# Two batches of x, the gate's weights and the tables are asked for later in the start-up of a hybrid attention and expert kernel

## The reference

```
x = x + attn_a(layernorm(x))   # 16 heads; q and k of width 8 + 32 rotary-like features r, v of width 8, softmax, Wo
x = x + ffn(layernorm(x))      # gate softmax over 8 experts, top 1, silu(x W1 + b1) W2 + b2, times the gate's weight
x = x + attn_b(layernorm(x))   # 16 heads, two softmaxes of width 8 per head, rotary tables, probs = p1 - lam * p2
x = x + ffn(layernorm(x))
```

## Time and profile before

| what | value |
| --- | --- |
| median of 3 runs | 1569.77 us (1566.09 to 1571.79) |
| the profiled execution's own time | 1582.06 us |
| its span | 1580.3 us |
| mean granted TensorE clock | 0.962 |
| PE busy | 1425.1 us (90%) |
| DVE busy | 1170.7 us (74%) |
| ACT busy | 1078.4 us (68%) |
| POOL busy | 704.4 us (45%) |
| DMA | 192.78 MB, mean 122 GB/s |

### The profile page before, as it was taken

How to read it: one execution, slowest core, us unless ns; L and a number is a source line. 1 busy time by engine, 2 the same in 40 slices (tenths; PEclk the granted TensorE clock), 3 DMA queues, 4 the chain that set the end, 5 groups by cost and what they waited for, 6 DMA issues and landing times.

```text
span 1580.3 us, 27271 instructions
## 1 busy us (share of the span) xinstructions
PE 1425.1 (90%) x9388; PEld 614.0 (39%) x9388; DVE 1170.7 (74%) x2030; ACT 1078.4 (68%) x1807; POOL 704.4 (45%) x770
## 2 busy tenths in 40 slices
PE   3999999999999998999999999998898889999946
PEld 1333333335554332555443223222232225554536
DVE  4777788777777678567777888788889895677234
ACT  1576666766655776777787787687877777777712
POOL 3412533342414755675648652242521017755633
PEclk8999999999999998999999998799999998999969
DMA  6674455756734145875211210201202044523222
GB/s 190 196 208 136 138 172 163 238 170 202 222 94 103 54 154 166 259 234 171 89 36 35 87 41 21 75 28 42 61 21 80 23 157 157 167 86 126 95 102 82
DMA packets 123743, 192.78 MB, mean 122 GB/s; under 512 B 16392, under 2 KB 91938, under 8 KB 123606
## 3 DMA queue, kind: packets, MB, share of 16 engines
q1 hardware_dynamic: 114296, 176.69, 37.7%
q0 software_dynamic: 6016, 12.71, 2.3%
q10 hardware_dynamic: 3294, 1.64, 0.4%
HBM read 120.59 MB, written 71.81 MB: 122 GB/s over the span
## 4 chain that ended last, share of the span: by engine, by line
PE 67%; DVE 11%; ACT 6%; issue 5%; POOL 5%; DMA 4%; SPq 0%; ACTq 0%; POOLq 0%; DVEq 0%
PE ps L1142 19%; PE ps L1108 11%; PE ps L1129 10%; DVE Mb L1485 7%; PE ps L1239 5%; PE ps L1226 5%; ACT P L1333 5%; PE ps L1076 4%; PE ps L1150 2%; POOL ROW L1399 2%; PE ps L1223 2%; DMA xs<-ROW,slot 1%; PE ps L1237 1%; PE ps L1176 1%; POOL rs L1708 1%
## 5 line engine op out<-in xcount | busy, mean ns | idle before, releaser
L1485 DVE TENSOR_REDUCE Mb<-ps 128x2 f32<-128x1024 f32 (+1 forms) x950 | 940.6, 1015 | 254.1 <-PE ps L1108 248.8
L1333 ACT ACTIVATE P<-ps 128x512 f32<-128x512 f32 (+1 forms) x1089 | 804.7, 774 | 225.3 <-PE ps L1129 214.2
L1108 PE MATMUL ps<-STK 32*128 32x512 f16 (+1 forms) x1536 | 412.2, 391 | 44.6 <-DVE Mb L1485 16.4
L1129 PE MATMUL ps<-STK 32*128 32x512 f16 (+1 forms) x1536 | 422.8, 389 | 29.3 <-ACT P L1333 18.6
L1142 PE MATMUL ps<-P,V 128*32 128x512 f32 x3072 | 420.7, 620 | 3.5 <-ACT P L1333 3.0
L1108 PEld LDWEIGHTS ps<-STK 32*128 32x128 f16 (+1 forms) x1536 | 103.7, 94 | 295.4 <-issue 99.5
L1129 PEld LDWEIGHTS ps<-STK 32*128 32x128 f16 (+1 forms) x1536 | 108.6, 94 | 257.5 <-issue 80.3
L1753 POOL DMA_INDIRECT xs<-ROW,slot x64 | 63.3, 989 | 126.9 <-DVE slot L1575 111.0
L1760 POOL TENSOR_TENSOR TH<-TH,Z 128x512 f32<-128x512 f32 x58 | 73.6, 1269 | 88.6 <-ACT Z L1379 88.3
L1142 PEld LDWEIGHTS ps<-P,V 128*32 128x32 f32 x3072 | 61.1, 109 | 116.0 <-issue 97.5
L1226 PEld LDWEIGHTS ps<-XT,WE 128*128 128x128 f32 x696 | 93.9, 196 | 4.1
(11 more groups left out here) (169 smaller groups left out, 1433.7 us busy)
## 6 DMA issues: line engine op xcount, KB each, us to landing
WE<-in_we SPq DMA_DIRECT2D x87, 576.0 KB, 4.2
STK<-qka SPq DMA_DIRECT2D x62, 480.0 KB, 6.1
qka<-HL SPq DMA_DIRECT2D x96, 256.0 KB
STK<-qkb SPq DMA_DIRECT2D x64, 256.0 KB, 2.6
qkb<-HL SPq DMA_DIRECT2D x96, 128.0 KB
X<-xs SPq DMA_DIRECT2D x77, 129.5 KB, 3.0
xs<-pad SPq DMA_DIRECT2D x8, 1036.0 KB, 8.1
qka<-HL SPq DMA_DIRECT2D x48, 128.0 KB
```

The lines of the kernel that those rows point to most:

```text
L1108: mm = eng.matmul(ps[:, bank + i, :], l_, r_, start=True, stop=True)
L1129: mm = eng.matmul(ps[:, bank + i, :], l_, r_, start=True, stop=True)
L1333: eng.activation(P[:, st % 3, j:j + n, :], ps[:, bank:bank + n, :], ACT.Exp, scale=SCALE_A if g < 4 * B else SCALE_B).then_inc(sem("exp"), 1)
L1485: eng.tensor_reduce(Mb[:, g % 2, at:at + 4 * n - 3:4], ps[:, bank:bank + n, :], AX, ALU.max).then_inc(sem("mx"), 1)
```

## The change

In `setups()`, the job that orders the loads, setup(4), setup(5) and setup(6) wait in the plan for the end of stack(0). No instruction is added or taken away and no semaphore wait is added: only the orders that `schedule()` writes out change.

```diff
@@ -363,6 +363,8 @@
         for i, n in enumerate((1, 4, 1, 1, 1, 1, 5, 2, NS, 4, 2)):
             if i == 3:
                 yield from after(("setup", (2,)))
+            if i in (4, 5, 6):
+                yield from after(("stack", (0,)))
             if i == 8:
                 yield from after(("mput", (3,)))
             yield from do(ranks[i], "setup", i, us=0.6 * n)
```

## The result

| | kernel before | changed kernel |
| --- | --- | --- |
| median | 1570.78 us (4 runs, 1566.09 to 1581.8) | 1592.8 us (4 runs, 1589.2 to 1600.57) |
| profiled execution: own time, span, mean granted clock | 1582.06, 1580.3, 0.962 | 1593.27, 1591.5, 0.957 |
| busy PE, DVE, ACT, POOL | 1425.1, 1170.7, 1078.4, 704.4 us | 1421.4, 1169.3, 1079.3, 704.7 us |

The ratio is 1.0111, 95% interval 1.006 to 1.0161: slower, as forecast, and by more. The medians are 22 us apart (17 by the ratio) and the two profiled executions 11.2 us. Forecast were 11.7 us; 1592.8 lies above the range, which ended at 1586.

What follows compares the result with a forecast made beforehand. The start was taken as bound by DMA up to 36 us, then by DVE's rowmax. Loads 0, late x 10.75 and clock 1.0 gave +11.7 us on the 1569.77 median: 1581.5 us, range 1573 to 1586.

Steps and rivals of the forecast that it cites:

- What bounds the kernel now: Start of the kernel: DMA sets the pace up to 36 us, then DVE's ten rowmax, 11.41 us, from 37.11 to 48.5.
- What moving the loads gives: nothing.: At put(0): x loads and tables ahead held up neither its issue nor its data; 0 us, at most -1.3.
- put(4) and put(5), a gain that nobody waits for: SP's queue: these puts leave some 2 us earlier, unread by group 0; stack(0) up to 0.5 us later at no cost.
- x of batch 2 is late: DVE's rowmax wait behind ln_stats for x, landing at 47.3, and for POOL; seventh rowmax and feat(6) 10.75 us later.
- TensorE's clock: PE's stall of 8 us halves the clock for part of the feat; +1.0 us after slack at stack(4), ends 0 and +4.
- What stays hidden: Later stack(3), WG, CS and ln_apply(3) cost 0, covered by other work; uncovered, stack(3) would cost 4 us.
- The sum: Whole kernel: 0 + 10.75 + 1.0 = +11.7 us, on the median of 1569.77 giving 1581.5 us.
- x past the stacks: Rival: SP's queue order does not bind, x lands at 40.5; +3.9 us less up to 1.2, 1572.5 to 1574; chance 0.12.
- the loads were not in the way: Denies the rival that the loads held up group 0, a 1.3 us gain, alone 1568.5; chance of a gain 0.02.
- Absorbed later: Rival: slack in groups 1 to 3 shrinks the +11.7 to a few us; chance 0.07.
- Longer than forecast: Rival: clock at 0.50 for all feat and x issues held by a full queue; 3 to 5 us more, 1585 to 1587; 0.07.
- How the numbers follow: Chances and range: forecast 0.72, x landing 46 to 48.5 (+9.4 to +12), clock 0 to +4; over 0.5% slower 0.78.

Runs made afterwards that it cites:

- dve_only: Kernel before with DVE's order of the changed kernel, x of batches 2 and 3 asked for early; 1582.81 us, ratio 1.0053.
- x_last: Changed kernel with stack(3) moved ahead of the x loads in SP's queue; 1599.33 us, one run.
- spread_puts: Kernel before with the two slow dimensions of the six DMAs of put(0) and put(1) swapped, columns reordered to fit; 1578.52 us, ratio 0.9965.
- spread_tables_late: As spread_puts, with the gate's weights and tables, not x, asked for behind stack(0); 1580.57 us, ratio 0.9992.
- again: Changed kernel once more, unedited, on chip 12, against the kernel before; 1584.86 us, ratio 1.0038.
- again_2: Changed kernel once more, unedited, on chip 8, against the kernel before; 1602.43 us, ratio 1.0146.
- same_as_before: Kernel before, unedited, measured against itself; 1576.6 us, ratio 1.0019.
- x_before_stacks: Changed kernel with the x loads ahead of stack(1) and stack(2), behind the puts of batch 0; 1582.4 us, ratio 1.0044.

## Why the prediction was right, and where it was wrong

- **What bounds the kernel now**, DMA up to 36 us and DVE's rowmax behind it: right. dve_only and x_last delay the rowmax and TensorE follows; spread_puts makes DMA faster and the first rowmax starts 4.8 us earlier.
- **What moving the loads gives: nothing.** Right: 6.76 us from put(0) to fhi(4) against 6.73, and spread_tables_late gains nothing either. The idle twelve engines of the earlier trace rows were the reason, as spread_puts shows.
- **put(4) and put(5), a gain that nobody waits for**: true, but it has a price of its own. stack(0) landed later, +0.46 us in the changed kernel (up to 0.5 was given), and +2.01 where x is early (dve_only).
- **x of batch 2 is late**: right in mechanism and size. Landing by 48.06 (forecast 47.3), wait 7.00 (6.8), POOL 1.42 (1.4), together +11.43 against 10.75. The error of 0.7 is the landing's: forecast 0.76 too early, less 0.1 for ln_stats(3).
- **TensorE's clock**: +1.0 net was taken. What the gap at group 4 holds beyond the rowmax is +1.3 in the profiled execution, +1.1 in again and +1.6 in again_2. The size is right, but the way to it is only in part: the slack at stack(4) was to take most of the clock's cost back. PE waits for stack(4) 0.80 us in the profiled execution, and there it takes back 0.4 of 1.7; in again and again_2 PE waits 1.36 and 1.23 us, as long as before, and it takes back nothing.
- **What stays hidden**: right; behind group 0 the chains of waits of both kernels hold the same eight waits for a DMA, the one for stack(4) among them.
- **The sum**, as far as it counts the start, was 11.7 us; the traces show 12.68, 12.76 and 12.96 at group 4, and the runs of again at equal granted clock, with its own stall added, 12.4.
- **The rivals.** x past the stacks fell (x at 48.06, not 40.5) and the loads were not in the way. Absorbed later fell for the first 190 us. Longer than forecast gave the right side, with the wrong reason: the clock was back within the features, and no issue was held back for long.
- **How the numbers follow** is the step that failed. The prediction put what TensorE's clock does behind the start at nothing, in the sum and in the range: all uncertainty went into the start, +9.4 to +12 and up to 4 for the clock there, with "a little for the spread of the runs". In its place the runs showed five places between groups 32 and 84 where the traces lie 9 to 11 us apart each, executions of one kernel over 28 us (1563.12 to 1591.5), and ratios of the changed kernel from 1.0038 to 1.0146 at one and the same gap of 12.7 to 13.0 us. In the measured set the medians are 22 us apart, 10 more than the forecast. That these 10 us were made by the clock is not shown for this set: the clocks of its runs of the kernel before are not on record, and its one pair of traces ends at +11.07. The signs stood in the profile of before: its execution was 12.3 us above the median at a mean clock of 0.962, and its trace has 28 us at half clock far from the change (the rows at the end). A range of 12.3 us to either side, 1569 to 1594, would have followed from that execution, and 1592.8 lies just inside it.

## What to carry to other kernels

A load that is moved behind others in a queue lands behind them: count the landings that stand ahead of it and their pace, then look for what is queued, on the engine that waits, behind the waiting instruction; here seven rowmax waited for two loads that cost nothing where they were. Before taking loads out of the way of a slow DMA, see whether the DMA engines are busy at all, since a DMA with a short slowest dimension leaves most of them idle and wants another shape. And where TensorE's clock falls in some executions and not in others, compare marks within the traces, which repeat within 0.5 us at the start of this kernel, and give the end a range as wide as two executions of one kernel are apart.

## What the runs showed of the hardware that was not expected

- The granted clock falls to 0.50 in the middle of busy work, in the same program in one execution and not in the next: between the outputs of groups 56 and 60 the profiled kernel before lost 9.3 us and same_as_before none. Of the profiled kernel before and of the changed kernel, the same 28 us after the start (the changed kernel is 20 us behind in its work at group 56, and 11 at group 60, so the instructions are not the same):

```profile
976.00:1004.00 28.00, 26.12 (x128) 4.36 (x132) 18.66 (x33) 15.04 (x27) 4.13 (x5) 0.51 0.13 38
```

```profile
976.00:1004.00 28.00, 24.83 (x191) 9.66 (x187) 24.16 (x52) 20.71 (x36) 5.39 (x7) 1.00 0.07 21
```

  PE is busy 26.12 of 28 us at 0.51 and runs 128 matmuls; at 1.00 it runs 191. One hundredth of the mean clock is worth 12.0, 11.5 and 11.8 us in the three sets.
- The time that SP needs to issue a DMA depends on the DMAs ahead of it: it issued put(2) and put(3) from 20.10 to 27.90 us in the kernel before and from 19.77 to 23.44 in spread_puts, the same six DMAs behind put(0) and put(1) of another shape.
- stack(0), on ACT's queue, lands later when SP's queue has asked for more ahead of it: 4.5 and 6.2 us to landing before, 5.3 and 8.0 in dve_only, 6.0 and 7.5 in x_before_stacks.
